# Attention with paged keys: ScalarE copies the own-key probabilities of four units at once, the mask is made in the third step, and the own keys are transposed behind an odd unit's scores

## What is computed

```python
q = rope(rmsnorm(x @ Wq.T)); k = rope(rmsnorm(x @ Wk.T)); v = x @ Wv.T
kc = k_cache[block_table].reshape(bsz, 512, HK, D)      # 16 pages of 32 keys
k_all = concatenate([kc, k], axis=1)                    # 512 cached and 32 own keys
scores = einsum('bqhd,bkhd->bhqk', q, repeat(k_all, 4, axis=2)) * SCALE
scores = where(valid, scores, -1e30)                    # cached keys beyond cache_seqlens
probs = softmax(scores)                                 # 32 query heads, 8 key heads
o = einsum('bhqk,bkhd->bqhd', probs, repeat(v_all, 4, axis=2))
x = x + o.reshape(bsz, seqlen, HQ * D) @ Wo.T
```

## Time and profile before

| | us |
|---|---|
| median of 3 runs | 2537.75 |
| lowest and highest run | 2532.34, 2540.56 |
| span of the profiled execution | 2632.1 |
| attention without its ends, 960 to 2220 us | 1260 |
| TensorE busy in these 1260 us | 1186.41 |

### The profile page before, as it was taken

One profiled execution on the slowest core, in us unless ns is written; L12 is line 12 of the kernel. 1 busy time (PEld: TensorE's weight loads), 2 busy tenths in 40 slices (PEclk: granted clock), 3 DMA queues, 4 the chain that ended last, 5 costly groups with the idle time before them and its releaser, 6 DMA issues. The chain is left out here.

```text
span 2632.1 us, 55771 instructions
## 1 busy us (share of the span) xinstructions
PE 2449.5 (93%) x16326; PEld 2204.1 (84%) x16327; DVE 1799.6 (68%) x3690; ACT 1587.4 (60%) x3313; POOL 643.5 (24%) x932
## 2 busy tenths in 40 slices
PE   6799899999999889999999999999999999499999
PEld 5688688888888789999999998999999999388887
DVE  6445438999898967777777777777777776544443
ACT  3222237777787777777777777777777776311111
POOL 1222030000000134434443444344433442000000
PEclk9899899999999989999999999999999999799999
DMA  6422432333334388887888888887888883766664
GB/s 230 143 78 76 147 125 85 117 99 99 112 101 131 112 290 275 276 274 261 267 284 272 263 269 272 283 265 259 278 277 267 264 271 133 269 208 215 218 216 152
DMA packets 376143, 541.56 MB, mean 206 GB/s; under 512 B 49395, under 2 KB 263091, under 8 KB 372211
## 3 DMA queue, kind: packets, MB, share of 16 engines
q1 hardware_dynamic: 303922, 316.33, 37.9%
q0 software_dynamic: 70016, 221.30, 24.5%
q10 hardware_dynamic: 2112, 2.89, 0.4%
HBM read 442.06 MB, written 98.30 MB: 205 GB/s over the span
## 5 line engine op out<-in xcount | busy, mean ns | idle before, releaser
L1298 ACT ACTIVATE att_prob<-att_prob,att_shift 128x544 f32<-128x544 f32 x512 | 383.2, 748 | 262.2 <-DVE att_shift L1319 239.8
L1597 PE MATMUL both_ps_o<-att_pt,att_v 128*128 128x128 f32 x4096 | 540.0, 275 | 0.0
L1597 PEld LDWEIGHTS both_ps_o<-att_pt,att_v 128*128 128x128 f32 x4096 | 504.9, 191 | 0.0
L1319 DVE CUSTOM_DVE_ANT_0 att_prob<-both_ps_s,att_mask 128x544 f32<-128x544 f32 x512 | 365.5, 714 | 0.0
L101 PE MATMUL both_ps_s<-att_k_hi,att_q_hi 128*128 128x272 f32 x1024 | 340.5, 333 | 6.7 <-DVE att_k_lo L1293 5.2
L1293 DVE TENSOR_TENSOR att_k_lo<-att_k_raw,att_k_hi 128x1024 fp32r<-128x1024 f32 (+1 forms) x320 | 337.8, 1055 | 2.0 <-ACT att_k_hi L1287 1.9
L1476 ACT ACTIVATE att_pt<-both_ps_pt 128x512 f32<-128x512 f32 x512 | 296.8, 580 | 47.0 <-remote 43.6
L1574 PE MATMUL both_ps_pt<-both_ident,att_prob 128*128 128x128 f32 x2048 | 309.2, 274 | 7.6 <-ACT att_prob L1298 6.0
L1508 DVE COPY att_p_own<-att_prob 128x32 f32<-128x32 f32 x512 | 91.9, 180 | 324.6 <-PE both_ps_s L103 154.9
L1412 POOL DMA_DIRECT2D att_vo<-v_own x256 | 140.1, 547 | 651.8 <-PE both_ps_o L1600 589.1
L103 PE MATMUL both_ps_s<-att_k_hi,att_q_lo 128*128 128x272 f32 x1024 | 297.8, 291 | 0.0
(11 more groups left out here) (191 smaller groups left out, 5169.0 us busy)
## 6 DMA issues: line engine op xcount, KB each, us to landing
att_k_raw<-in_k_pages SPq DMA_DIRECT2D x1024, 128.0 KB, 3.9
q_t<-qkv_out_t SPq DMA_DIRECT2D x128, 256.0 KB
att_q_raw<-q_t POOLq DMA_DIRECT2D x64, 512.0 KB, 7.1
o_t<-att_o POOLq DMA_DIRECT2D x64, 512.0 KB, 6.9
out_o<-o_t SPq DMA_DIRECT2D x32, 1024.0 KB, 6.7
out_inv<-inv_t SPq DMA_DIRECT2D x32, 1024.0 KB, 6.7
qkv_w_stage<-in_w_qkv SPq DMA_DIRECT2D x12, 1024.0 KB, 5.2
l_w_stage<-in_w SPq DMA_DIRECT2D x8, 1024.0 KB, 6.8
```

Source lines behind the costliest of these rows:

```text
L1298: act.activation(prob[:, b, :], prob[:, b, :], ACT.Exp, bias=shift[:, b:b + 1], scale=-1.0, accum_out=total[:, j // HK, j % HK:j % HK + 1] ...
L1319: dve.tensor_tensor_reduce(out=prob[:, b, :].rearrange("p (a n) -> p a n", a=2), in0=ps_s[:, j % 2, :, 0:HALF], in1=mask[:, j // HK, :].re ...
L1597: pe.matmul(out, v_sb[p][:, c, h * DH:(h + 1) * DH], pt_sb[:, j % OG, c, :], start=(c == 0), stop=False)
```

## The change

1. `gather` moves from VectorE (eight copies of 128x32 in a half) to ScalarE (two copies of 128x128 in a half, in steps 1 and 5, behind `hi_part` and ahead of `copy_pt`). VectorE now waits for `gathered` before it masks u(4) and u(8), whose buffer holds the first unit of the gathered four. In the place of the copy that used to carry the waits of `mask_and_max`, VectorE runs a memset of 128x1 into a tile that nobody reads.
2. The own keys' transpose moves on TensorE from the end of steps 3 and 7 to the place right behind the scores of u(5) and u(9). It writes spare columns of `ps_s[:, 0]` instead of `ps_s[:, 1]`, and waits for one masked unit less. It has a semaphore of its own, `own_t_done`.
3. `copy_own` moves from the start of VectorE's steps 4 and 0 to behind `mask_and_max` in steps 3 and 7; the scores that wait for it are now those of u(6) and u(10) (steps 4 and 0) instead of u(7) and u(11) (steps 5 and 1).
4. The sums are inverted (128x8) on VectorE in step 6, before the transpose, and step 7 copies the transposed 8x128 reciprocals.
5. `make_mask` moves from step 6 to the end of step 2, and its wait to the next sequence's first `mask_and_max`.
6. In layer 0 two blocks of loads of adapter numbers get bounds checks (eight more rows each on TensorE's sequencer). Two semaphores of the mask in layers 1 and 2 are one now.

```diff
@@ def scores
-        if j % OG == 3 and later(u, OG + 3):
+        if j % OG == 2 and later(u, OG + 2):
             pe.wait_ge(pto_ready, UNITS // OG * i + j // OG)
-        if h == 3 and later(u, HK + 3):
+        if h == 2 and later(u, HK + 2):
             pe.wait_ge(inv_ready, 2 * i + p)
@@ def spare
-        return ps_s[0:rows, 1, half, D - P:D]
+        return ps_s[0:rows, 0, half, D - P:D]
@@ def mask_and_max
+        dve.memset(ahead_of_max[:, b:b + 1], 0.0)
@@ scalar
+        def gather(i, u, g):
+
+            act.wait_ge(exp_done, u + 1)
+            if later(u, 2 * OG):
+                act.wait_ge(own_t_done, UNITS // OG * i + g - 1)
+            act.activation(p_own[:, g % 2, :, :], prob[:, :, NKEY:NALL], ACT.Copy).then_inc(gathered, 1)
...
+                if j % OG == 1:
+                    gather(i, u + 2, j // OG)
                 copy_pt(u, j)
@@ vector
             if j % HK == 0:
-                make_mask(dve, s, j // HK)
+                dve.wait_ge(lens_and_masks, s + 2)
+            if later(u, NB_P):
+                if j % OG == 0:
+                    dve.wait_ge(gathered, UNITS // OG * i + j // OG)
+                dve.wait_ge(t_done, u - NB_P + 1)
             dve.wait_ge(s_done, u + 1)
-            if later(u, NB_P):
-                dve.wait_ge(t_done, u - NB_P + 1)
-
-        def gather(u, j):
-
-            dve.wait_ge(exp_done, u + 1)
-            dve.tensor_copy(p_own[:, j // OG % 2, j % OG, :], prob[:, j % NB_P, NKEY:NALL]).then_inc(gathered, 1)
...
         def invert(i, p):
 
-            dve.wait_ge(t_done, UNITS * i + HK * (p + 1))
+            dve.wait_ge(exp_done, UNITS * i + HK * (p + 1))
+            dve.reciprocal(inv_q[:, p, :], total[:, p, :]).then_inc(inverted, 1)
+
+        def copy_inv(i, p):
+
+            dve.wait_ge(own_t_done, UNITS // OG * i + HK // OG * (p + 1))
             if later(i, 1):
                 dve.wait_ge(inv_stored[p], 16 * i)
-            dve.reciprocal(inv_sb[:, p, :], spare(0, HK)).then_inc(inv_ready, 1)
+            dve.tensor_copy(inv_sb[:, p, :], spare(0, HK)).then_inc(inv_ready, 1)
...
-                if j % OG == 0 and later(u, OG):
-                    copy_own(*group_before(i, j, 1))
-                    if j % HK == 0:
-                        invert(*group_before(i, j, 1)[:1], (1 - p))
...
+                if j % HK == HK - 2:
+                    invert(i, p)
+                if j % OG == 3:
+                    copy_own(i, j // OG)
+                if j % HK == HK - 1:
+                    copy_inv(i, p)
...
+                if j % HK == 2 and not (last and p):
+                    make_mask(dve, s + 1, 1 - p)
@@ tensor
+        def transpose_own(i, u, j, last):
+
+            p, g = j // HK, j // OG
+            if not (last and j == UNITS - 1):
+                pe.wait_ge(masked, u + 2)
+            pe.wait_ge(gathered, UNITS // OG * i + g + 1)
+            mm = pe.transpose(spare(1, P), p_own[:, g % 2, :, :].rearrange("p u k -> p (u k)"), ident[:, :])
             if j % HK == HK - 1:
-                mm = pe.transpose(spare(0, HK), total[:, p, :], ident[:, :])
-            mm.then_inc(t_done, 1)
+                pe.wait_ge(inverted, 2 * i + p + 1)
+                mm = pe.transpose(spare(0, HK), inv_q[:, p, :], ident[:, :])
+            mm.then_inc(own_t_done, 1)
...
                     scores(pe, i + (j + 2) // UNITS, u + 2, (j + 2) % UNITS)
+                if j % OG == OG - 1:
+                    transpose_own(i, u, j, last)
                 if j >= OG:
                     outputs(i, u - OG, j - OG)
```

More of the change, by code:

```diff
@@ L189, in layer0, with entries @@
         y_stored = m.sems("y_stored", XB)
-        def entries(buf, first, n, engine, top):
+        def entries(buf, first, n, engine, top, waited=False):
             return nc.values_load_multi_w_load_instructions(
                 buf[0:1, bass.ds(first, n)], engines=[engine], min_val=0, max_val=top,
-                skip_runtime_bounds_check_because="the sort gives places within these")[1]
+                skip_runtime_bounds_check_because=None if waited else "the sort gives places within these")[1]
         def tiles(eng, body):
@@ L433, in tile @@
                         n = XB if is_tile(XB * (i + 1)) else NT0 % XB
-                        adapters[:] = entries(adapter, XB * i, n, mybir.EngineType.PE, NAD0 - 1)
+                        adapters[:] = entries(adapter, XB * i, n, mybir.EngineType.PE, NAD0 - 1,
+                                              waited=not later(XB * i, NAD0))
                     multiply(XB * i + j, j % 2, adapters[j])
@@ L1218, in attention @@
     mask, prob = rest.sb("mask", [P, 2, NALL]), rest.sb("prob", [P, NB_P, NALL])
-    shift, total = rest.sb("shift", [P, NB_P]), rest.sb("total", [P, 2, HK])
+    ahead_of_max = rest.sb("ahead_of_max", [P, NB_P])
+    shift, total, inv_q = rest.sb("shift", [P, NB_P]), rest.sb("total", [P, 2, HK]), rest.sb("inv_q", [P, 2, HK])
     rest.reach(AFTER_TAIL)
@@ L1234, in attention @@
     masked = m.sem("masked")
-    exp_done, gathered = m.sem("exp_done"), m.sem("gathered")
-    t_done = m.sem("t_done")
+    exp_done, gathered, inverted = m.sem("exp_done"), m.sem("gathered"), m.sem("inverted")
+    t_done, own_t_done = m.sem("t_done"), m.sem("own_t_done")
     pt_ready, pto_ready = m.sem("pt_ready"), m.sem("pto_ready")
@@ L1539, in pair @@
                 u, s, p = UNITS * i + j, 2 * i + j // HK, j // HK
[L1540 to L1543 removed]
                 if not (last and j >= UNITS - 2):
[L1545 to L1548 removed]
+                    wait_for_scores(i + (j + 2) // UNITS, 2 * i + (j + 2) // HK, u + 2, (j + 2) % UNITS)
                     mask_and_max(dve, u + 2, (j + 2) % UNITS)
+                if j % HK == HK - 2:
[4 more added lines that the diff above has]
+                    copy_inv(i, p)
                 if not later(u, HK - 1):
@@ L1567, in tensor, with transpose @@
     def tensor(pe):
-        def transpose(u, j, last):
-            p, g = j // HK, j // OG
+        def transpose(u, j):
             pe.wait_ge(exp_done, u + 1)
@@ L1574, in transpose @@
                 mm = pe.transpose(ps_pt[:, j % 2, c, :], prob[:, j % NB_P, c * P:(c + 1) * P], ident[:, :])
-            if j % OG == OG - 1:
-                if not (last and j == UNITS - 1):
-                    pe.wait_ge(masked, u + 3)
-                pe.wait_ge(gathered, u + 1)
-                mm = pe.transpose(spare(1, P), p_own[:, g % 2, :, :].rearrange("p u k -> p (u k)"), ident[:, :])
+            mm.then_inc(t_done, 1)
+        def transpose_own(i, u, j, last):
[4 more added lines that the diff above has]
+            mm = pe.transpose(spare(1, P), p_own[:, g % 2, :, :].rearrange("p u k -> p (u k)"), ident[:, :])
             if j % HK == HK - 1:
-                mm = pe.transpose(spare(0, HK), total[:, p, :], ident[:, :])
-            mm.then_inc(t_done, 1)
+                pe.wait_ge(inverted, 2 * i + p + 1)
+                mm = pe.transpose(spare(0, HK), inv_q[:, p, :], ident[:, :])
+            mm.then_inc(own_t_done, 1)
         def outputs(i, u, j):
@@ L1613, in pair @@
                     outputs(i - 1, u - OG, UNITS - OG + j)
-                transpose(u, j, last)
+                transpose(u, j)
             if last:
```

25 lines of the change are left out of this document (9 added, 16 removed).

## The result

| | before | after |
|---|---|---|
| median of the timed runs | 2539.07 us (2532.34 to 2540.56) | 2553.95 us (2552.14 to 2555.07) |
| ratio after / before, 95% | | 1.0064 [1.0052, 1.0076] |
| span of the profiled execution | 2632.1 us | 2551.8 us (its own time 2553.36) |
| predicted | | 2553, 2528 to 2578 |

The account below looks back on a forecast made before the run. The prediction took TensorE to bound the kernel, with no gap in the timed runs. The median 2537.75 us plus a 15.4 us stall in step 4 gave 2553 us, range 2528 to 2578.

Parts of the forecast that it names:

- The bound: In attention TensorE sets the end; a half in the timed runs is 18.8 us of its work, nothing left to gain.
- The stall of step 4: Scores of u(6) wait for copy_own: TensorE idles 0.24 us in each of 64 halves, 15.4 us; 2553 us, chance 0.45.
- The other waits: The remaining new waits, such as the own keys' transpose in step 3 and step 7's copies, are met in time.
- The 94 us: Profiled span 2632.1 us against median 2537.75: 94.35 us, laid to step 7's gap, present only under the profiler.
- the sum 1.55 x 62: Mean half 20.32 us less gap-free half 18.77, times 62 halves: 96 us, separating the profiled execution from the median.
- the gap ahead of L101: Sign in the changed kernel's profile: step 7's TensorE gap now stands before the scores instead of the transpose.
- Gap in the timed runs: Rival: step 7's scores wait 0.20 us longer, step 4's stall is swallowed; 11 us slower, 2549 us, chance 0.15.
- Faster, since the small copies cause the late news: Rival: without VectorE's small copies step 7's gap goes, up to 70.5 us gained; 2467 to 2530 us, chance 0.18.
- Hidden: Rival: step 4's chain ends at 7.03 to 7.10 us, so no change; 2538 to 2543 us, chance 0.22.

Follow-up runs that it names:

- near copy: The kernel before with only layer 0's bounds checks and the merged mask semaphores: 2635.72 us on chip A, ratio 1.0006.
- the kernel with two masks: The changed kernel with a second mask of 448 columns, into a tile nobody reads, ahead of make_mask in step 2: 2664.6 us on chip A, ratio 1.0118.

## Why the prediction was right, point by point

**The bound.** TensorE bounds, and idle time ahead of it is lost nearly one for one: a half of the changed kernel is 19.04 - 18.79 = 0.25 us longer than with the mask in step 5, 63 halves make a mask, and 0.25 x 63 = 16 us. The profiled spans of the two differ by 2551.8 - 2536.6 = 15.2 us; forecast were 15.4.

**The stall of step 4.** Forecast 0.24 us x 64 = 15.4 us; measured 2.69 - 2.42 = 0.27, x 63 = 17.0 us, with timed differences of 14.9 to 19.2. Three experiments (the mask moved, ScalarE's copy moved, the copies back on VectorE) bring step 3 back to 2.42. Link by link, from the start of u(3)'s scores (1506.79):

| start of | forecast | measured |
|---|---|---|
| mask of u(3) | 1.13 | 1.05 |
| exponential, high part, ScalarE's copy | 1.88, 2.62, 3.57 | 1.81, 2.56, 3.51 |
| memset | 3.88 | 4.04 |
| mask of u(4), low part, `make_mask` | 3.97, 4.61, 5.75 | 4.08, 4.73, 5.87 |
| mask of u(5) | 6.30 | 6.27 |
| `copy_own`, its end | 6.94, 7.22 | 6.92, 7.21 |
| scores of u(6) | 7.27 | 7.35 |
| the same without a wait | 7.03 | 7.02 |

In this half the stall is 7.35 - 7.02 = 0.33 us; it is one of the longer ones. Several links were mis-sized and nearly cancel, so that the total came out this close is in part luck. From the end of ScalarE's copy (1510.59) to VectorE's memset are 0.24 us, not 0.02: this handover had been taken as free, by VectorE's own next start. In return the masks cost less. The mask of u(3) starts 0.08 earlier; the memset takes 0.04 ahead of the mask of u(4) instead of 0.09, and nothing ahead of the mask of u(5) instead of 0.06; `make_mask` takes 0.40 to the next start instead of 0.49. (No row gave the forecast's lower bound of 0.03 for the memset; it was a guess, and the memset comes out below it at u(5).) The last link is 0.11 from `copy_own`'s end to the load, not 0.05, and the product starts 0.03 behind the load.

The 0.24 us are not the way from one engine to the other. VectorE's waits for `gathered` and `t_done` stand on register operations of their own ahead of the memset, as the order of step 2 in the section on the change shows, and these run only after the copy has ended:

```profile
L1516 DVEq ALU_OP  x1: 40/40/40, 1510.6 to 1510.6; - x1
...
L1517 DVEq ALU_OP  x1: 40/40/40, 1510.7 to 1510.7; - x1
```

The trace has L1516 at 1510.63, 0.03 behind the copy's end, L1517 at 1510.71 and the memset at 1510.83. The next half has only one of the two operations (L1517 at 1529.69, the memset at 1529.81), and there the memset follows the copy by 0.15. The two kinds of half alternate, and step 3 follows them: 2.74 us in the 30 halves with two operations, 2.65 in the 31 with one, in all four traces of the changed kernel. So one such operation costs 0.09 us, and here TensorE pays it in full. With the mask in step 5 the same 0.24 and 0.15 us are there, and step 3 is 2.42 in both kinds: the chain has room then. Where the wait stands on the instruction itself the way is short: from VectorE's `att_shift` to the exponential it takes 0.04 (1513.79 to 1513.83).

The two new operations by form:

```profile
L1486 ACT ACTIVATE att_p_own<-att_prob 128x128 f32<-128x128 f32 x124 | 37.4, 302 | 4.3
...
L1314 DVE TENSOR_SCALAR att_mask<-att_key_at,att_lens_f 128x512 f32<-128x512 f32 x62 | 29.8, 481 | 0.0
L1320 DVE MEMSET att_ahead_of_max<- 128x1 f32 x496 | 29.3, 59 | 87.3 <-ACT att_p_own L1486 76.9 <-PE both_ps_s L103 10.3
```

The copy takes 0.30 us (forecast 0.29), the memset's record 0.06.

**The other waits.** They hold as computed: step 7 is 2.53 us, as it is in the kernel with before's order and no gap (item 1 alone, 2.52). Item 6 costs nothing, as said.

**The 94 us.** Here the forecast was right for half a wrong reason. The timed runs that were compared have no gap, as it took them to have none, and the sum 1.55 x 62 did separate the two kinds of execution. But it isn't the profiler that makes the difference. On chip A the timed runs of before take 2634.41 us and its near copy spans 2633.3 under the profiler; elsewhere spans and times agree at about 2537. So an execution has the gap or doesn't, profiled or not, and the trace of before came from one like those on chip A. The prediction named only the profiler and left this case out. That it is the chip is argued and not shown: all runs on chip A were made at one time, so the chip can't be told from whatever else was particular to that time. With the profiler goes the forecast that the changed kernel's profile shows the gap ahead of L101: its four traces all come from executions without one.

**What names the wait.** I expected `att_pto` as the releaser and the profile says `att_shift`. The load waits for both; `att_shift` was there at 1513.79, the copy ended at 1514.00, the load began at 1514.11, so it was the copy that held it. In the kernel with two masks the row reads `att_pto`.

**The rivals.** *Gap in the timed runs:* on chip A the wait does move from the transpose to the scores, as that rival says, and the gap stays (72.4 us against 70.1). Its price was too high: a half takes 20.39 to 20.40 us there against 20.35, some 0.05 more instead of 0.20, because step 7 gets only 0.10 longer (4.11 to 4.12 us against 4.01) and step 0 gets 0.08 shorter. And it called step 4's stall swallowed; with two masks three quarters of it remained. By that the changed kernel should lose some 0.2 us a half on chip A too (an estimate, three quarters of 0.27), which no run shows. *Faster, since the small copies cause the late news:* false where it was tried. On chip A the gap is there in full with the copies gone from VectorE, and on the other chips there is none with them. So the small copies are not its cause, and what the prediction drew for them from the rule of the Trainium skill (SBUF — State Buffer, section Who interferes with whom) did not happen. VectorE's low parts and `make_mask`, which go from SBUF to SBUF too, stay in every kernel; no run tests whether they and GpSimd get in each other's way. *Hidden:* the chain ends some 0.3 us too late for that.

**Still open:** why news of TensorE's finished work comes some 2 us late on chip A in step 7, whether that belongs to the chip, and what the changed kernel itself takes there. None of the variants is faster than the kernel before by more than its interval: with item 1 alone a half takes 18.78 us, and between 960 and 2140 us the profile lists no wait of TensorE, so what is left is TensorE's own work.

## What to carry to other kernels

When a change moves work off an engine, follow the longest chain through the wait that it leaves behind, link by link with starts instead of busy times, and hold its end against the start of the instruction that needs it: here 0.27 us at the end of 7.3 us of links was the whole result. Count every handover between engines as a link (0.04 us here where the wait stands on the instruction itself), and every wait on a register operation of its own as one more (0.09 us here): they run after the news has come. Ahead of trusting a gap in a trace, see whether the span agrees with the timed median; if it doesn't, compare on one chip before explaining.

## What the runs showed of the hardware

- The same kernel took 2634.41 us on one chip (27 runs) and 2535.93 to 2537.35 on four others, steadily within each, at a granted clock of 0.98 on all. In the traces the difference is in attention: step 7 takes 4.01 instead of 2.52 us and step 0 2.40 instead of 2.31, so a half takes 20.35 instead of 18.78.
- VectorE's maximum reaches ScalarE's exponential 0.04 us after the end of its record. ScalarE's copy reaches VectorE's memset after 0.15 us where one register operation that carries a wait stands between, and after 0.24 where there are two. From VectorE's `copy_own` to TensorE's weight load are 0.11 us.
- A memset of 128x1 on VectorE takes 59 ns, and adds nothing that shows where VectorE waits for nothing (the mask starts at 1513.06, the memset's record at 1513.09).
- Inverting the sums as 128x8 takes 0.20 us on VectorE, against 0.93 as 8x128:

```profile
L1529 DVE RECIPROCAL att_inv_q<-att_total 128x8 f32<-128x8 f32 x62 | 12.2, 197 | 0.0
```
